# A graph network of attention and three layers: the first layer step's weights, aggregation, first residual and means moved into the attention's last step, and its norm ahead of the last attention norm

## What is computed

```python
x = layernorm(x + relu(attention(x, adj)) @ Wo)
h0 = x
for l in range(3):
    si, sj = x @ attn_w[l, :d], x @ attn_w[l, d:]
    scores = si[:, :, None] + sj[:, None, :] + attn_b[l]
    scores = where(scores >= 0, scores, 0.2 * scores)
    attn = softmax(where(mask, scores, -inf))
    h = layernorm(x + attn @ x) * g1[l] + beta1[l]
    ff = gelu(h @ W1[l] + b1[l]) @ W2[l] + b2[l]
    x = layernorm(h + ff) * g2[l] + beta2[l]
out = layernorm(h0 + x)
```

## Time and profile before

| | us |
|---|---|
| median of three runs | 1644.83 |
| the profiled execution | 1644.53 |
| its span, first to last instruction | 1642.70 |
| TensorE busy, share of the span | 98% |
| VectorE, GpSimd busy, share of the span | 81%, 81% |
| ScalarE busy, share of the span | 75% |
| the attention block ends, the layer block begins, from the span's start | 364.26 |
| first matmul of the first feed-forward product | 386.84 |

### The profile page before, as it was taken

The page is one execution under the profiler, slowest core; times in us unless marked ns, Lnnn a source line. Parts: engine busy times, 40 slices in busy tenths (PEclk is TensorE's granted clock), DMA queues, the critical chain, the costliest instruction groups (busy, mean ns, idle before and its releaser), DMA issues.

```text
span 1642.7 us, 40121 instructions
## 1 busy us (share of the span) xinstructions
PE 1613.5 (98%) x12036; PEld 1437.1 (87%) x12036; DVE 1329.5 (81%) x5321; ACT 1232.8 (75%) x2856; POOL 1329.7 (81%) x2367
## 2 busy tenths in 40 slices
PE   9999999978999999999999999999999999999997
PEld 8888888867898998989899898998889899998986
DVE  5999999987777777788877777778888888888875
ACT  6888898876777677776767777677677778787874
POOL 7788888856778787777878777787878999999996
PEclk9999999999999999999999999999999999999999
DMA  7334322212123121211213222121211222222211
GB/s 229 104 103 141 100 92 90 90 40 91 48 94 102 38 77 38 77 60 55 77 40 102 64 76 70 45 77 39 77 41 63 77 77 77 77 89 84 83 46 58
DMA packets 141721, 127.62 MB, mean 78 GB/s; under 512 B 12240, under 2 KB 132560, under 8 KB 141648
## 3 DMA queue, kind: packets, MB, share of 16 engines
q1 hardware_dynamic: 141648, 126.81, 24.3%
HBM read 89.04 MB, written 37.75 MB: 77 GB/s over the span
## 4 chain that ended last, share of the span: by engine, by line
PE 73%; DVE 3%; POOL 1%; issue 0%; ACT 0%; POOLq 0%; DVEq 0%; ACTq 0%
PE ps L45 33%; PE ps L979 30%; PE ps L951 5%; PE ps L965 3%; DVE gnn_junk L1111 2%; PE ps L943 1%; PE ps L958 1%; DVE gnn_e L1144 0%; POOL n L169 0%; DVE gnn_res L1174 0%; DVE xo L1222 0%; DVE res L1154 0%; POOL gnn_inv_last L913 0%; ACT gnn_w_hi L1067 0%; DVE gnn_st L1178 0%
## 5 line engine op out<-in xcount | busy, mean ns | idle before, releaser
L979 PE MATMUL ps<-gnn_w_hi,gnn_g_hi 128*128 128x256 f32 x1536 | 434.2, 283 | 1.5 <-DVE gnn_res L1174 1.5
L979 PE MATMUL ps<-gnn_w_lo,gnn_g_hi 128*128 128x256 f32 x1536 | 429.3, 279 | 0.0
L979 PE MATMUL ps<-gnn_w_hi,gnn_g_lo 128*128 128x256 f32 x1536 | 429.0, 279 | 0.0
L1079 ACT ACTIVATE gnn_g_hi<-ps,b_cols 128x512 fp32r<-128x512 f32 x384 | 264.3, 688 | 199.3 <-PE ps L45 199.3
L1182 DVE TENSOR_TENSOR gnn_g_lo<-ps,gnn_g_hi 128x512 fp32r<-128x512 f32 x384 | 262.8, 684 | 109.9 <-ACT ps L1080 109.8
L45 PE MATMUL ps<-gnn_hT_hi,gnn_w_hi 128*128 128x512 f32 x768 | 338.0, 440 | 0.0
L45 PE MATMUL ps<-gnn_hT_lo,gnn_w_hi 128*128 128x512 f32 x768 | 303.8, 396 | 0.0
L45 PE MATMUL ps<-gnn_hT_hi,gnn_w_lo 128*128 128x512 f32 x768 | 303.6, 395 | 0.0
L979 PEld LDWEIGHTS ps<-gnn_w_hi,gnn_g_hi 128*128 128x128 f32 x1536 | 289.0, 188 | 3.9 <-DVE gnn_res L1174 1.7
L979 PEld LDWEIGHTS ps<-gnn_w_lo,gnn_g_hi 128*128 128x128 f32 x1536 | 289.1, 188 | 2.2
L979 PEld LDWEIGHTS ps<-gnn_w_hi,gnn_g_lo 128*128 128x128 f32 x1536 | 289.0, 188 | 0.0
(11 more groups left out here) (145 smaller groups left out, 3995.2 us busy)
## 6 DMA issues: line engine op xcount, KB each, us to landing
x<-hist SPq DMA_DIRECT2D x49, 512.0 KB, 3.9
hist<-xo SPq DMA_DIRECT2D x48, 512.0 KB, 4.1
aw<-in_L_gnn_attn_w SPq DMA_DIRECT2D x48, 256.0 KB, 4.2
gmask<-mask_hist SPq DMA_DIRECT2D x48, 256.0 KB, 4.1
att_xT_raw<-in_xT SPq DMA_DIRECT2D x16, 512.0 KB, 3.3
att_xl<-in_x SPq DMA_DIRECT2D x16, 512.0 KB, 3.5
gnn_fin<-hist SPq DMA_DIRECT2D x15, 512.0 KB, 3.8
out<-gnn_fin SPq DMA_DIRECT2D x15, 512.0 KB, 3.0
```

The source lines that it names most:

```text
L979: mm = e.matmul(FF2[j % 2], g[a][:, m, j * N:(j + 1) * N], W2[b][:, m, :], start=(n == 0), stop=(n == len(terms) - 1))
L1079: e.activation(g[0][:, m, :], FF1[FFB[m]], ACT.Gelu, bias=bias)
```

## The change

All that layer step 0 needs ahead of its norm is moved into the attention's last step (j is the graph in it), and its PSUM tiles are now the projections' banks, A[0] and A[1]. Its tensors (u, top, small, e1, pT, st1, mv1 and others) are allocated ahead of both blocks, and the two memsets of ones (L838) are moved to the attention's start on GpSimd. In the layer block step 0's instructions are gone, with the keep_running of 40; VectorE makes the weights of step 1 first and the two parts of split_w1_lo behind. On GpSimd the norm of step 0 (up to n1) comes first, then the last attention norm, the first half of first_w2_lo, hb, and the other half. The sync queue's code isn't changed.

```diff
 # TensorE, attention
+                def first_spread_sj():
+                    e.wait_ge(sums_set, 4 * GROUP)
+                    e.wait_ge(proj_out, 6 * NG)
+                    for j in range(GROUP):
+                        mm = e.transpose(FIRST_TB[:, j * N:(j + 1) * N], first_s[0][1][:, j:j + 1].to_broadcast([P, N]), ident[:])
+                    mm.then_inc(sjT_made, 1)
+
+                def first_probs_T():
+                    e.wait_ge(p_out, 1)
+                    for j in range(GROUP):
+                        mm = e.transpose(FIRST_TB[:, j * N:(j + 1) * N], e1[:, j, :], ident[:])
+                    mm.then_inc(gpT_made, 1)
+
+                def first_aggregate(j):
+                    if j == 0:
+                        e.wait_ge(x_ones, 2)
+                        e.wait_ge(gpT_out, 1)
+                    if j >= 2:
+                        e.wait_ge(y1_out, j - 1)
+                    e.matmul(FIRST_AGG[j % 2][:, 0:XW], pT[:, j, :], gx[0][:, j, :], start=True, stop=True).then_inc(agg_made, 1)
                 def body(q, par, a1, a2, before=True):
                     for j, i, has1, (has2, t2, par2, j2) in graphs(q, par, a1):
+                        if not a1 and j == 0:
+                            first_spread_sj()
+                        if not a1 and j == 3:
+                            first_probs_T()
                         e.wait_ge(exped, 2 * i + 1)
...
                 steps(e, body, first=1)
+                first_aggregate(0)
+                first_aggregate(1)
                 output_product(B - 1, False)
+                first_aggregate(2)
+                first_aggregate(3)
 # ScalarE, attention: at the end of graph j of the last step
+                        if not a1 and j == 1:
+                            first_exps()
+                        if not a1 and j == 3:
+                            first_copy_pT()
 # VectorE, attention: at the end of graph j of the last step
+                        if not a1 and j == 0:
+                            first_masked_sums()
+                            first_shifts()
+                        if not a1 and j == 2:
+                            first_probs_max()
...
                 body(NG // 2 - 1, 1, False, False)
+                first_residual1(0)
+                first_residual1(1)
+                first_stats1(0)
+                first_stats1(1)
                 residual(NG // 2 - 1, B - 1, 1, GROUP - 1, True)
+                first_residual1(2)
+                first_residual1(3)
+                first_stats1(2)
+                first_stats1(3)
+                first_mean_variance1()
                 statistics(B - 1, 1, GROUP - 1)
 # GpSimd, layers
-                e.wait_ge(stored[1], START + 16 * (NG // 2 - 1))
-                ln_group(e, NG - 1, 1)
...
                     e.wait_ge(n1_out, t1 + 1)
+                    if isinstance(t1, int) and t1 == 0:
+                        e.wait_ge(stored[1], START + 16 * (NG // 2 - 1))
+                        ln_group(e, NG - 1, 1)
+                        first_w2_lo(slice(0, FT // 2))
+                        e.wait_ge(aff_set, 1)
...
-                first_w2_lo()
                 ln_attention(0, 0)
+                first_w2_lo(slice(FT // 2, FT))
 # TensorE, layers
-                first_spread(0)
+                first_spread(1)
                 keep_running(e, FF1[0], 24)
-                probs_T(0)
-                for j in range(GROUP):
-                    aggregate(0, 0, j)
-                first_spread(1)
-                keep_running(e, FF1[0], 40)
                 transpose_h(0, HT_FIRST)
                 keep_running(e, FF1[0], 24)
 # ScalarE, layers
                 split_w1_hi(0)
-                exps(0)
                 split_w2_hi(0)
-                copy_pT(0)
                 exps(1)
                 hT_hi(0, HT_FIRST)
 # VectorE, layers
-                masked_sums(0, 0, 0)
-                attention_shifts(0, 0, first_s[0][0])
-                split_w1_lo(0, 0)
-                probs_max(0)
-                split_w1_lo(0, 1)
-                for j in range(GROUP):
-                    residual1(0, 0, j)
-                    stats1(0, j)
-                mean_variance1(0)
                 masked_sums(1, 1, 0)
                 attention_shifts(1, 1, first_s[1][0])
+                split_w1_lo(0, 0)
+                split_w1_lo(0, 1)
                 probs_max(1)
                 hT_lo(0, HT_FIRST)
                 for j in range(GROUP):
```

More of the change, by code:

```diff
@@ L398, in _ @@
                 score_mask(0, 0)
+                for par in range(2):
+                    e.memset(gx[par][:, :, D:XW], 1.0).then_inc(x_ones, 1)
                 xT_hi(1, 1)
@@ L528, in exps, with first_exps, first_copy_pT @@
                     ins.then_inc(exped, 1)
+                def first_exps():
+                    e.wait_ge(bias_out, 1)
+                    for j in range(GROUP):
+                        e.activation(e1[:, j, :], u[:, j, :], ACT.Exp, bias=small[:, 2, j:j + 1])
+                        ins = e.activation(FIRST_TB[:, j * N:(j + 1) * N], u[:, j, :], ACT.Exp, bias=small[:, 3, j:j + 1], scale=0.2)
+                    ins.then_inc(exp_out, 1)
+                def first_copy_pT():
+                    e.wait_ge(gpT_made, 1)
+                    e.copy(pT[:].rearrange("p j n -> p (j n)"), FIRST_TB).then_inc(gpT_out, 1)
                 def body(q, par, a1, a2):
@@ L622, in first_sum, with first_masked_sums @@
                                            accum_out=first_s[t][n][:, j:j + 1]).then_inc(sums_set, 1)
+                def first_masked_sums():
+                    e.wait_ge(m_ld[0], 32)
+                    hold_dve(e, sjT_made, 1)
+                    for j in range(GROUP):
+                        ins = e.tensor_tensor_reduce(out=u[:, j, :], in0=FIRST_TB[:, j * N:(j + 1) * N], in1=gmask[0][:, j, :],
+                                                     scale=1.0, scalar=LOWEST, op0=ALU.add, op1=ALU.max,
+                                                     accum_out=top[:, j:j + 1])
+                    ins.then_inc(u_out, 1)
@@ new lines, in first_probs_max, with first_residual1 @@
+                def first_probs_max():
+                    e.wait_ge(exp_out, 1)
+                    e.tensor_tensor(e1[:].rearrange("p j n -> p (j n)"), FIRST_TB, e1[:].rearrange("p j n -> p (j n)"),
+                                    ALU.max).then_inc(p_out, 1)
+                def first_residual1(j):
+                    bank = FIRST_AGG[j % 2]
+                    e.wait_ge(agg_made, j + 1)
+                    e.reciprocal(grden[:, j:j + 1], bank[:, D:D + 1]).then_inc(recip_out, 1)
+                    e.wait_ge(recip_out, j + 1)
+                    e.scalar_tensor_tensor(out=y1[:, j, :], in0=bank[:, 0:D], scalar=grden[:, j:j + 1],
+                                           in1=gx[0][:, j, 0:D], op0=ALU.mult, op1=ALU.add).then_inc(y1_out, 1)
@@ L624, in body, with first_stats1, first_mean_variance1 @@
+                def first_stats1(j):
+                    e.wait_ge(y1_out, j + 1)
+                    e.bn_stats(st1[:, j, :], y1[:, j, :]).then_inc(bn1_out, 1)
+                def first_mean_variance1():
+                    hold_dve(e, bn1_out, GROUP)
+                    for j in range(GROUP):
+                        ins = e.bn_aggr(mv1[:, j, :], st1[:, j, :])
+                    ins.then_inc(mv1_out, 1)
                 def body(q, par, a1, a2, before=True, early=None):
@@ L881, in ln_ffn, with first_w2_lo @@
                     e.wait_ge(x_out, t + 1)
-                def first_w2_lo():
+                def first_w2_lo(parts):
                     hi, lo = V[0]
                     e.wait_ge(w2_hi_set, 1)
-                    for m in range(FT):
+                    for m in range(FT)[parts]:
                         ins = e.tensor_tensor(lo[:, m, :], w2_raw[:, m, :], hi[:, m, :].bitcast(F32), ALU.subtract)
-                    ins.then_inc(w2_split, 1)
+                    if parts.stop == FT:
+                        ins.then_inc(w2_split, 1)
                 def final_sum(t, par, half):
```

48 lines of the change are left out of this document (31 added, 17 removed).

## The result

The changed kernel takes **1657.21 us** (median of four runs, 1656.75 to 1657.61) against 1645.03 (1644.46 to 1645.35): ratio **1.0076**, 95% interval 1.0063 to 1.0088. It is slower by 12.2 us; the forecast was 1650.2 with a range to 1654.5. The profiled execution took 1656.75, its span 1654.96, 12.2 more than before's 1642.72.

What follows compares the result with a forecast made beforehand. TensorE is busy 98% of the span; the seam between attention and first layer step is set by a four-engine chain. m = 3 +4.4 and clock +1.3 give +5.7 on 1644.53: 1650.2 us, range 1643.3 to 1654.5.

Steps and rivals of the forecast that it cites:

- Step 1: Attention's last step: work moved onto nearly full VectorE makes it 8.3 us longer, bounds 5.5 and 10.5.
- Step 2: First layer's start: first feed-forward matmul at 383.2, 3.6 us earlier than before.
- T: Forecast start of the layer block, 364.3 + 8.3 = 372.6 us.
- Step 3: Sync queue: step 2's loads, behind the last norm and store, delay VectorE's sums; TensorE's m = 3 starts 4.4 us later.
- Step 4: Clock after TensorE's 8 us wait at m = 3: a half-clock stretch of 3.3 us costs 1.3, bounds 0 and 1.7.
- Parts at nothing: w2's split, the attention-start memsets and the removed filler transposes: no cost, though memsets 0.15 us if their cover is gone.
- the rivals: Faster 1640.9, chance 0.08; no change 1646.6, 0.26; slower by more 1652.4 or 1653, 0.16; start bound by w2's split.

Runs made afterwards that it cites:

- e1: Changed kernel with the loads of step 2 issued ahead of the sync queue's wait for the last attention norm; 1647.79 us, ratio 1.0021 to the kernel before.
- e10: Changed kernel with the layer block's tensors back at the addresses of the kernel before; 1653.37 us, ratio 1.0047 to the kernel before.
- e4: Kernel before without the keep_running of 40 in the seam; 1645.89 us, ratio 1.0007.
- e3: Kernel before with only the change's allocation: weights 6400 bytes up, res2, norm, hb, hT and g 128; 1649.73 us, ratio 1.0031.
- e5: Kernel before with the weights and junk allocated 6272 bytes up, hb, hT and g unmoved; ratio 1.0028.
- e6: Kernel before with a pad ahead of res2, so res2, norm, hb, hT and g lie 128 bytes up, weights unmoved; ratio 1.0028.
- e12: Kernel before with a pad of 128 bytes directly ahead of g, so only g and the small tiles behind it move; ratio 1.0012.
- e7: Kernel before with the change's allocation and 1792 bytes more pad: weights 8192 bytes up, hT and g 1920; ratio 1.0027.
- e11: e10 plus the load order of e1, filler transposes in the attention's last step, and step 2's first graph's sums ahead of hT_lo; 1640.75 us, ratio 0.9976.

## Why the prediction was wrong

The direction was right, the size wasn't: +12.2 measured, +5.7 forecast.

- **Step 1, right.** Block 8.1 us later, and 8.4 from the probsT copy on (29.05 against 343.72 to 364.38, 20.66, before); forecast 8.3. VectorE waited for TensorE where I said. That it came out so close is in part luck. The copy beside the affine addition took 1.1 us longer, not 0.3; attT_lo was done at 366.9, where I had 365.85, or 366.45 with the 0.6 for the clock; and what stood behind it took 5.5 us instead of 6.15. TensorE was at half clock for 10.2 us of the last step, where I had one stretch of 3.3 and, in the upper bound, two.
- **Step 2, right.** First product at 383.72 against 383.2. n1 was done at T + 6.5 instead of 5.8: one normalization met both w1 subtractions and took 2.65 us, and the four took 4.26 where I had 3.8. The Trainium skill, SBUF — State Buffer, section SBUF: two separate sides, has VectorE and GpSimd take turns on a shared pair of ports for a whole instruction; this trace agrees, with 4.26 against 2.17 us, and 0.93 against 0.41 for a sum.
- **Step 3, mechanism right, 1.0 too small.** Store 383.04 (382.8), landed 9.6 behind it (9.0), sums 4.0 (3.9), m = 3 at 397.40 (396.4). e1 shows that this is the queue's order. From the fit in the Trainium skill, DMA: Bandwidth & Descriptors, section Anatomy of one DMA, which is for one transfer of GpSimd's queue, I had estimated 7.2 us for this line of transfers (7.4, again an estimate by that page, with a KB of 1024 bytes); the trace has 9.6.
- **Step 4, mechanism right, mis-sized.** I took the stretch of 3.3 us from the earlier trace rows, which stands behind a wait of 1.83 us. Behind a wait of 8.36, 4.85 us of work ran at 1.2 GHz: +2.35 (10.65 against 8.30 from m = 3 to the second product) instead of +1.3, and above my bound of 1.7. In e10, behind a wait of 8.39, it was 5.45 us of work.
- **Parts at nothing, the step that failed.** I priced the split of w2, the memsets and the fillers. The split was done in time (394.73, forecast 394.6). That the fillers were free isn't shown: e4 has 1.4 us for them in the kernel before, and the changed kernel was not run with them. The part of the change that I did not even list was the allocation: it cost 4.4 us of 12.2 (e3: 5.3 by itself, e10: 3.8 when taken back). The change's own text says that these tensors are allocated ahead of both blocks. In the sum it stands behind the sentence that all later steps follow with TensorE full, so that what is lost stays lost: I took for granted that 45 untouched steps keep their 1170.3 us, and they took 1174.5.

Together: 1.0 + 1.05 + 4.4 is the 6.5 by which I was off. Without the allocation's cost the result is e10's 1653.4, within my range. None of the rivals had the allocation in it.

## What to carry to other kernels

When an engine's work is moved ahead of another's, look at what stands in the queues behind the work that is now later: here a store that nobody was in a hurry for had the next step's loads behind it, and they cost more than the move gained at the first product. Price the allocation too. Where a kernel is full of matmuls, add a padding of 128 bytes in a run of its own before you put a difference of 0.3% down to the edit.

## What the runs showed that I had not expected

- The pace of matmuls depends on the distances between SBUF tensors: 1170.3 us for 45 layer steps, 1175.1 with 128 bytes between the weights and the activations, 1169.6 with 128 bytes ahead of both. The Trainium skill, SBUF — State Buffer, section SBUF: two separate sides, says of TensorE's access to SBUF that it never waits on another engine; it says nothing of where tensors lie, and from that sentence alone one wouldn't expect e3, e5 and e6 to cost anything. The measurement decides; whether the matmuls wait for anyone, or what else slows them, was not found.
- The length of a wait doesn't tell how long the half clock lasts. It was longest around the longest waits, 10.24 us around 8.36 (changed kernel) and 6.02 (e4). But around a wait of 1.83 at the layers' start it was 3.41 us in before, e5 and e12 and 6.83 in e6 and e7, and around one of 3.53 in the changed kernel 6.83, while e11 has 3.41 with one of 3.62.
- A transfer's landing depends on what is in flight: aw 4.2 us behind x alone, 6.8 behind the store, fin and x.
